# An adaLN transformer block on one core: ranking the first batch over two batches, freeing the last attention group, and gathers that name fewer rows

## What is computed

```python
h = _layernorm(x) * (1 + ca) + sa
q = (h @ Wq + bq).reshape(b, heads, dh, t)          # k, v the same
attn = softmax(einsum('bhdt,bhds->bhts', k, v) * temperature)
out = einsum('bhdt,bhts->bhds', q, attn)
x = x + ga * out.reshape(b, t, d)
h = _layernorm(x) * (1 + cb) + sb
scores = einsum('bsd,d->bs', h, w_router)
top_scores, top_idx = top_k(scores, T // 2)
selected = take_along_axis(h, top_idx)
processed = gelu(selected @ W1 + b1) @ W2 + b2
x = x + gb * h.at[top_idx].add(sigmoid(top_scores) * processed)
```

## Time and profile before

| | us |
|---|---|
| median of 3 runs | 2358.24 |
| lowest, highest | 2357.28, 2362.88 |
| the profiled execution | 2358.23 |
| its span, first to last instruction | 2356.5 |
| attention, first row maximum to the first FFN matmul | 56.0 to 1654.46 |
| FFN | 1654.46 to the end |

### The profile page before, as it was taken

One profiled execution on the slowest core, in us unless ns is written; L12 is line 12 of the kernel. 1 busy time (PEld: TensorE's weight loads), 2 busy tenths in 40 slices (PEclk: granted clock), 3 DMA queues, 4 the chain that ended last, 5 costly groups with the idle time before them and its releaser, 6 DMA issues.

```text
span 2356.5 us, 40955 instructions
## 1 busy us (share of the span) xinstructions
PE 2267.9 (96%) x12790; PEld 880.6 (37%) x12790; DVE 1909.5 (81%) x2909; ACT 1488.0 (63%) x2622; POOL 1238.9 (53%) x1111
## 2 busy tenths in 40 slices
PE   7999999999999999999999999897979999999998
PEld 3333333333333333333333333331434444444443
DVE  5999999999999999999999999998844653663543
ACT  2888888888888888888888887777411111111111
POOL 4667666677666766667766676554513222212300
PEclk9999999999999999999999999999989999999999
DMA  7333343333333334333333333223422021111100
GB/s 238 82 73 78 77 98 75 78 92 71 85 93 73 79 77 98 73 78 93 71 88 89 73 79 80 68 57 113 135 72 63 24 63 50 43 43 50 59 19 18
DMA packets 121342, 180.57 MB, mean 77 GB/s; under 512 B 43737, under 2 KB 43737, under 8 KB 120577
## 3 DMA queue, kind: packets, MB, share of 16 engines
q1 hardware_dynamic: 111152, 152.03, 26.4%
q0 software_dynamic: 9728, 25.23, 3.5%
q10 hardware_dynamic: 208, 0.28, 0.1%
HBM read 67.18 MB, written 43.16 MB: 47 GB/s over the span
## 4 chain that ended last, share of the span: by engine, by line
PE 54%; DVE 22%; issue 11%; POOL 5%; ACT 4%; DMA 2%; SPq 1%; DVEq 0%; ACTq 0%; POOLq 0%
DVE nmax L1040 16%; PE sc L755 13%; PE sc L768 13%; PE sc L567 10%; PE acc L614 10%; PE pj L589 6%; PE pj L577 3%; POOL x L1369 3%; ACT probs L840 2%; DVE stats L1070 1%; DVE x L1065 1%; DVE qn L1088 1%; DMA router_row<-in_L_ffn_w_router 1%; ACT room L813 1%; DVE rinv L1083 1%
## 5 line engine op out<-in xcount | busy, mean ns | idle before, releaser
L840 ACT ACTIVATE probs<-sc,nmax 128x1024 f32<-128x1024 f32 x1024 | 1137.6, 1116 | 238.8 <-DVE nmax L1040 233.6
L1040 DVE TENSOR_REDUCE nmax<-sc 128x1 f32<-128x1024 f32 x1024 | 1217.3, 1213 | 53.4 <-PE sc L567 47.3
L614 PE MATMUL acc<-probs,qn 128*32 128x512 f32 x4136 | 553.0, 607 | 8.6 <-DVE x L1065 6.9
L577 PE MATMUL pj<-room 128*128 128x512 f16 x1500 | 388.2, 382 | 5.4 <-DVE room L1004 5.0
L930 ACT ACTIVATE probs<-sc,b_col 128x512 f32<-128x512 f32 x128 | 88.0, 687 | 471.3 <-PE sc L755 442.4
L768 PE MATMUL sc<-room,probs 128*128 128x512 f16 x1536 | 352.1, 379 | 0.0
L567 PE MATMUL sc<-stacks 128*128 128x512 f16 x1024 | 308.8, 384 | 19.2 <-ACT probs L840 17.1
L567 PE MATMUL sc<-room 128*128 128x512 f16 x1024 | 308.7, 383 | 16.9 <-issue 7.2
L1249 DVE CAST probs<-probs 128x512 f16<-128x512 f32 x128 | 57.3, 448 | 257.1 <-ACT probs L930 191.3
L768 PEld LDWEIGHTS sc<-room,probs 128*128 128x128 f16 x1536 | 150.3, 98 | 181.3 <-issue 0.2
L577 PEld LDWEIGHTS pj<-room 128*128 128x128 f16 x1500 | 145.1, 98 | 189.3 <-ACT room L813 13.3
(11 more groups left out here) (162 smaller groups left out, 2241.6 us busy)
## 6 DMA issues: line engine op xcount, KB each, us to landing
stacks<-room SPq DMA_DIRECT2D x512, 64.0 KB
room<-room SPq DMA_DIRECT2D x508, 64.0 KB, 2.0
h_rows<-hbuf SPq DMA_DIRECT2D x132, 128.0 KB, 2.3
out<-base SPq DMA_DIRECT2D x132, 128.0 KB, 2.5
room<-in_L_attn_x SPq DMA_DIRECT2D x96, 128.0 KB, 2.6
rows<-mod_rows SPq DMA_DIRECT2D x32, 256.0 KB, 4.0
room<-in_L_ffn_W SPq DMA_DIRECT2D x8, 1024.0 KB, 5.2
probs<-in_L_wmod SPq DMA_DIRECT2D x4, 1024.0 KB, 13.5
```

The source lines that it names most:

```text
L577: mm = nc.tensor.matmul(dst, hT16[par][:, a, cc, p * P:(p + 1) * P], w[:, z, cc, :], start=(t == 0), stop=(t == len(terms) - 1))
L614: mm = nc.tensor.matmul(acc[at:at + DH, :], qn[:, (p // 2) % 2, p % 2, h2, :], probs[:, (2 * p + h2) % PROBS, half * D:(half + 1) * D], st ...
L840: nc.scalar.activation(probs[:, u % PROBS, :], slot(g, ring_at(p, h2)), ACT.Exp, bias=nmax[:, u % PROBS:u % PROBS + 1], accum_out=rsum[:, ...
L1040: nc.vector.tensor_reduce(nmax[:, u % PROBS:u % PROBS + 1], slot(g, ring_at(p, h2)), AX.X, ALU.max, negate=True).then_inc(max_done, 1)
```

## The change

1. *Ranking.* The loop runs over batches 0 to 5; batch 6 stands in code of its own like batch 7. `rank_first` is called in both, with groups numbered 0 to 7 over the two. It now puts the first fifteen parts (above of tile 0, then before and above of tiles 1 to 7 in turn) behind pairs 4, 8 and 12 of groups 0 to 4, weights and slots behind pairs 6 and 8 of group 5, which is group 1 of batch 7. SP loads the score row at the first group of batch 6.
2. *The kept numbers.* POOL stores batch 0's slots at the end of group 1 and early in group 2 of the last batch; SP loads them back in group 2, DVE reads them at pair 14 of group 2; the gather stands one wait earlier in the last group.
3. *The last group.* It has no statistics of x2, no router product at its end and no post-processing on POOL beyond the residual. These (for the group before the last) move to the FFN's first batch: statistics at step 1, products at step 6, POOL's part behind the gather of base rows and ahead of the slot stores of batch 1. SP waits for it behind weight load 5 in place of in the group.
4. *The FFN's first batch.* Tiles 2 to 7 of batch 1 stand at steps 1, 2, 3, 3, 4 and 5 (before 1, 1, 2, 3, 3 and 4); the last group's own statistics at step 6 (5), its products at 11 (9), ACT's exponential of scores at 12 (10), weights at 13 (12).
5. *Gathers.* They name rows up to the end of their own batch as source. POOL's wait for all stores stands ahead of the last gather, not of that of batch 1.

```diff
@@ SP
-            with sp.Fori(0, B - 1) as b:
+            with sp.Fori(0, B - 2) as b:
                 body(b, False)
+            body(LAST - 1, False)
             body(LAST, True)
...
-                    if last and g == 0:
-                        sp.wait_ge(s_sc, 16 * (B - 1))
+                    if first_rank and g == 0:
+                        sp.wait_ge(s_sc, 16 * (B - 2))
                         load_scores(0)
                     if last and g == GB - 1:
-                        load_kept(0)
...
                         replicate((g + 1) % 2, 0, b * GB * 4 + 4 * (g + 1) + 2)
+                        if last and g == GB - 2:
+                            load_kept(0)
                         replicate((g + 1) % 2, 1, b * GB * 4 + 4 * (g + 1) + 4)
-                    sp.wait_ge(post_done, b * GB + g + 1)
-                    store_rows(before[g], (g + 1) % 2)
+                    if not (last and g == GB - 1):
+                        sp.wait_ge(post_done, b * GB + g + 1)
+                        store_rows(before[g], (g + 1) % 2)
...
-            for j in range(4, 7):
+            for j in range(4, 6):
                 load_weights(j)
+            sp.wait_ge(post_done, NG)
+            store_rows(NG - 2, (NG - 2) % 2)
+            load_weights(6)
@@ DVE
+            RANK_AT = (4, 8, 12)
+
             def rank_first(g, p):
...
+                n = 3 * g + RANK_AT.index(p) if p in RANK_AT else None
+                if n == 0:
                     nc.vector.tensor_copy(r.s8[:], scores[:, AHEAD:AHEAD + TB]).then_inc(s_s8, 1)
                     dve.wait_ge(s_s8, 1)
                     dve.wait_ge(r.s_srow, 16)
                     count_above(nc, dve, r, 0, only)
+                elif n is not None and n < 2 * TB - 1:
+                    if n % 2 == 1:
+                        count_before(nc, dve, r, (n + 1) // 2, only)
+                    else:
+                        count_above(nc, dve, r, n // 2, only)
+                if g == GB + 1 and p == 6:
                     weights(slice(0, LAST * TB), 1)
+                if g == GB + 1 and p == 8:
                     dve.wait_ge(s_tok, 3)
                     find_slots(nc, dve, r, r.tokens[:, 0:TB, :], only)
...
-                        if end and p == 2:
+                        if last and g == GB - 2 and p == 14:
                             numbers(0)
...
-                        if p == 5 or p == 7:
+                        if (p == 5 or p == 7) and not end:
                             stats_of_x2(b, g, (p - 5) // 2)
...
-            TILES_AT = {0: (0, 1), 1: (2, 3), 2: (4,), 3: (5, 6), 4: (7,)}
+            TILES_AT = {0: (0, 1), 1: (2,), 2: (3,), 3: (4, 5), 4: (6,), 5: (7,)}
@@ POOL, the last batch and behind it
+                    if last and g == GB - 3:
+                        wait_alone(r.s_slot, 1)
+                        store_kept(nc, r, sel_rows, range(0, 2))
...
-            residual(B, 0)
             wait_alone(pv_done, ALL_PAIRS)
             gather_base(0, out_rows[0:T])
+            normed_before(LAST, GB - 1)
+            h_times(LAST, GB - 1)
+            h_plus(LAST, GB - 1)
+            residual(B, 0)
+            base_times(LAST, GB - 1)
+            base_plus(LAST, GB - 1)
             wait_alone(r.s_slot, 2)
             store_kept(nc, r, sel_rows, range(TB))
...
-                    else:
+                    if n == B - 2:
                         for i in range(2):
                             pool.wait_ge(s_st[i], 128 * (NG // 2 + i) + 16)
-                    gather_h(n + 1, h_rows)
-                    gather_base((n + 1) % 2, out_rows)
+                    gather_h(n + 1, h_rows[0:(n + 2) * T])
+                    gather_base((n + 1) % 2, out_rows[0:(n + 2) * T])
```

89 lines of the change are left out of this document (42 added, 47 removed).

## The result

| | before | after |
|---|---|---|
| median of the runs | 2359.89 us (7 runs, 2357.28 to 2362.88) | 2368.55 us (7 runs, 2362.41 to 2370.23) |
| ratio to before | | 1.0028, 95% interval 1.0016 to 1.0040 |
| profiled execution | 2358.23 us, span 2356.5 | 2370.23 us, span 2368.5 |

The changed kernel is 4 to 9 us slower. I had forecast 2346.3 us with a range up to 2355. The size of the loss lies around what a measurement can tell from no change; its sign is settled, and it is not the sign I gave.

What follows compares the result with a forecast made beforehand. TensorE, busy 96% of the span, was taken as the bound, with VectorE bounding the last batch's first three groups. Terms 1.7 + 4.3 + 4.8 + 1.1 = 11.9 us off 2358.2 gave 2346.3 us, range 2338 to 2355.

Steps and rivals of the forecast that it cites:

- Term 1: Loop one turn shorter: one of six jumps goes at a group's end, 1.7 us faster.
- Term 2: First ranking spread over five groups in place of three, so ties meet POOL's work differently: 4.3 us faster.
- Term 3: Last attention group: no wait for kept numbers, fewer slow matmuls, statistics of x2 moved out: 4.8 us faster.
- it is issued some 2.6 earlier; I take 0.8 of stall: Last group's first weight load: issued 2.6 us earlier, needing 5.2 to land, leaving ScalarE 0.8 us of stall.
- Rival (c): Last group stays nearly as long, weight load and ScalarE taking DVE's place: its gain 1 us, time 2350.1; chance 0.12.
- Term 4: First FFN batch: gather without the stores' wait but behind a later POOL queue, rows at +75, 1.1 us faster.
- POOL is free at +67.4: First FFN batch: POOL finishes slot stores and post-processing 67.4 us after the FFN's start and can gather.
- The rows are there 7.5 us behind the gather's first issue.: First FFN batch: batch 1's gathered rows land 7.5 us after first issue, at +75, before at +76.15.
- (a): First FFN batch: the gather's wait goes nearly whole, 8.1 us more gain, time 2338.2; chance 0.14.
- (b): Batch 6's ranking pays as the last batch did: a loss of 1.8 us there, time 2352.4; chance 0.15.
- (d): FFN's start: POOL's passes cost DVE their whole length, 11.9 us in place of 7, time 2351.3; chance 0.09.
- (e): First FFN batch: POOL's chain makes the kernel slower, with slots beyond +50; 2361 at +53; chance 0.04.

Runs made afterwards that it cites:

- experiment 1: Changed kernel with the last batch's scores' store moved a batch later, behind the gather of FFN batch 1: 2360.28 us, ratio to before 1.0003.
- experiments 7 to 9: Changed kernel with first weight load ahead of row stores: 2357.38 us; that plus late scores' store, post-processing unmoved: 2343.15 us; likewise, post-processing moved: 2353.31 us.
- experiments 1 and 5: The edit of experiment 1 on the changed kernel (2360.28 us), and on the kernel before with only the ranking and gather changes (2348.52 us).
- experiment 12: Kernel before with only the scores' store moved a batch later: 2354.42 us, ratio 0.9979.
- experiment 2: Changed kernel with GpSimd's wait for all stores of rows put back ahead of the gather for FFN batch 1: 2365.22 us, ratio 1.0026.

## Why the prediction was wrong

**Term 1 (-1.7) was right.** Batch 5's last group takes 48.56 us; one jump is gone.

**Term 2 (-4.3) was right as a sum.** In the profiled execution the seven groups give 2.6, with 49.7 to 53.8 us for the five ranking ones; in the kernel with ranking alone the seven take 358.7 us (-4.5). The ties' mean is 0.99 us, before 1.34. Its parts were off in both directions, which is luck: the group with weights and slots took 52.6 us (forecast 49.7; 51.4 in most other executions) and the one behind it 48.6 (47.5), the fourth and fifth ranking groups 49.7 and 51.6 (51 and 53). The kernel with ranking alone was 5.6 us faster where terms 1 and 2 said 6.0.

**Term 3 (-4.8) failed, at the step "it is issued some 2.6 earlier; I take 0.8 of stall".** The issue time was about right (5.8 us into the group, forecast 5.3). The landing time was not: I took the 5.2 us of the earlier trace rows, a median over loads that have no gather beside them. The change itself put the gather 9 us earlier, just ahead of this load, and the load took 9.9 us where it had taken 5.6 behind the same eight stores. Rival (c) named this place with some half of its size: it took 3.8 us off the term, and 6.7 were gone. Once the load goes first, the group takes 54.0 us and term 3 comes out as forecast (-4.7). Even then the moved post-processing pays little: the group is 55.8 us with it left in, so the move brings 1 to 2 of the 4.7 (experiments 7 to 9).

**Term 4 (-1.1) came out at +12.1, at two steps.**

- *"POOL is free at +67.4"*, so the gather starts then. GpSimd was free at +67.3, but the numbers were cast at +70.0, and the first issue is at +71.0. Their cast is queued on VectorE behind the gelu of step 10 and the last low half, that gelu behind ScalarE's last weight half (1715.58), and the load of that half behind the kept numbers, which wait for the late slot stores (8.25 us of idle time of ScalarE). In the kernel before, the stores' wait hid the time of the cast. I had followed GpSimd's queue and not the one that feeds it.
- *"The rows are there 7.5 us behind the gather's first issue."* They took 17.3. The 7.5 was read behind a wait that had emptied the DMA engines. With the wait gone the gather runs beside what it used to wait for: 7.0 us go to the scores' elements (experiment 1), 2.8 to the eight stores (experiments 1 and 5).

The forecast for the rows was +75 and they came at +88.3: 3.6 late in issue and 9.8 in landing. That is all of it. The slots were forecast well (ready at +37.5, forecast +38.3).

PE's stall ahead of the wait was mis-sized, but its place was right. I had forecast 2.5 us "inside the wait that remains"; it was 8.1 with the slower matmuls behind it. PE wanted W2's low half at 1684.75 and got it at 1689.4, since the half's split stands behind the delayed ties and subtractions. It lay inside the wait all the same: PE's product of step 10 ended at 1711.7, and its gelu started at 1717.40, behind the weight half. No run removes the stall alone; this is read from the order of the queues.

**The rivals.** (a) and (b) did not occur. Of (d), the exclusion of VectorE and GpSimd was sized right at 7 us, not 12: from the FFN's first matmul to the slots three subtractions take 4.5 us more than their 0.69 each and three ties 3.0 more than their 0.35, 7.5 in all. The trace agrees once more with the rule of the Trainium skill (SBUF — State Buffer, Who interferes with whom): the subtractions of 1675.01 and 1682.84 take 2.72 us in place of 0.69. (e), with a chance of 0.04, had the right sign by the wrong mechanism: it needed slots beyond +50. None of my cases let a transfer take longer because of another, though all terms with a transfer in them changed its company. A case of that kind deserved more chance than all my slower ones together.

What stays open: why the scores' elements hold up the completion of stores issued just ahead of them on the same queue (experiment 12), since the trace of the kernel before shows 0.04 of DMA share from 1715.6 to 1722, and why they did not in experiment 2. And I did not try the moved post-processing at a later place, behind the slot stores.

## What to carry to other kernels

A duration read behind a wait is the duration with that wait in place; when a change removes the wait or brings transfers together, price each transfer with its new company, and when the wait goes, look up the second-latest thing it hid. The order of issue is worth more than the moment: one 1 MB load ahead of a gather and eight stores gave 7 us, one 4 KB store behind a gather 1 to 6 by the ratios. And work freed from a group that is not bound by its engine must not be set down where that engine feeds the next critical chain.
